# Half of the K stack transfers are issued by ScalarE's queue

## What is computed

```python
x = x + tanh(g_xattn) * xattn(layernorm(x), ctx, Wq, bq, Wk, bk, Wv, bv, Wo, bo)
x = x + tanh(g_ffn) * moe(layernorm(x), Wr, br, w1, b1, w2, b2, Wp1, bp1, Wp2, bp2)
```

## Time and profile before

| what | us |
|---|---|
| median of three runs | 2294.24 |
| the profiled execution | 2282.05 |
| its span on the core | 2280.3 |
| attention (by the stretches of the trace, about) | 0 to 1740 |
| experts (about) | 1760 to 2280 |
| TensorE busy, whole span | 2146.6 (94%) |
| ScalarE busy, whole span | 1162.3 (51%) |

### The profile page before, as it was taken

The page is one execution under the profiler, slowest core; times in us unless marked ns, Lnnn a source line. Parts: engine busy times, 40 slices in busy tenths (PEclk is TensorE's granted clock), DMA queues, the critical chain, the costliest instruction groups (busy, mean ns, idle before and its releaser), DMA issues. The chain is left out here.

```text
span 2280.3 us, 61866 instructions
## 1 busy us (share of the span) xinstructions
PE 2146.6 (94%) x23534; PEld 1870.1 (82%) x23534; DVE 1414.3 (62%) x3219; ACT 1162.3 (51%) x2765; POOL 803.2 (35%) x1200
## 2 busy tenths in 40 slices
PE   5899999999999999999999999999993799999994
PEld 4688888888888888888888888888872678888883
DVE  4777777777777777777777777777743111111114
ACT  1366666666666666666666666666651223333330
POOL 4323433433433433443343343344211133333331
PEclk9999999999999999999999999999986899999996
DMA  5555555555555555555555555555403686777775
GB/s 137 146 132 151 138 139 138 134 148 137 132 137 139 146 139 141 134 139 144 136 131 139 150 134 144 134 135 137 125 19 104 209 270 187 218 220 218 210 222 158
DMA packets 253683, 345.06 MB, mean 151 GB/s; under 512 B 90280, under 2 KB 170508, under 8 KB 253260
## 3 DMA queue, kind: packets, MB, share of 16 engines
q1 hardware_dynamic: 222716, 304.93, 50.2%
q0 software_dynamic: 20256, 23.21, 5.2%
q10 hardware_dynamic: 10416, 12.98, 1.7%
HBM read 155.83 MB, written 42.86 MB: 87 GB/s over the span
## 5 line engine op out<-in xcount | busy, mean ns | idle before, releaser
L569 DVE TENSOR_REDUCE max_part<-max_ps 100x1 f32<-100x512 f32 (+1 forms) x1536 | 994.7, 655 | 349.2 <-PE max_ps L809 325.2
L452 ACT ACTIVATE probs<-score_ps 128x400 f32<-128x400 f32 (+1 forms) x1536 | 753.6, 503 | 427.6 <-PE score_ps L792 419.5
L792 PE MATMUL score_ps<-q_stack,k_stack 97*128 97x200 f32 (+1 forms) x3072 | 618.4, 284 | 4.6 <-ACT probs L452 3.4
L809 PE MATMUL max_ps<-k_stack,q_stack 96*100 96x512 f32 (+1 forms) x1536 | 597.2, 389 | 10.1 <-DVE max_part L569 9.6
L792 PEld LDWEIGHTS score_ps<-q_stack,k_stack 97*128 97x128 f32 (+1 forms) x3072 | 476.0, 184 | 78.0 <-issue 32.8
L389 POOL TENSOR_TENSOR ctx_hi<-ctx_raw,zero_col 128x256 fp32r<-128x256 f32 (+1 forms) x384 | 213.3, 586 | 467.7 <-PE v_ps L823 427.4
L859 PE MATMUL pv_ps<-probs,v_ones 128*17 128x100 f32 x12288 | 307.5, 253 | 0.6 <-ACT probs L452 0.6
L859 PEld LDWEIGHTS pv_ps<-probs,v_ones 128*17 128x17 f32 x12288 | 261.9, 99 | 45.1 <-issue 37.5
L809 PEld LDWEIGHTS max_ps<-k_stack,q_stack 96*100 96x100 f32 x1536 | 257.2, 167 | 21.6 <-DVE max_part L569 16.3
L1222 ACT ACTIVATE hid<-h_ps,b_c 128x256 f32<-128x256 f32 x245 | 116.0, 474 | 311.3 <-PE h_ps L1378 311.3
L1122 POOL DMA_INDIRECT results_by_token<-y_t,slot x98 | 152.9, 1561 | 343.1 <-DVE y_t L1329 185.3
(11 more groups left out here) (186 smaller groups left out, 2289.5 us busy)
## 6 DMA issues: line engine op xcount, KB each, us to landing
k_stack<-k_hl SPq DMA_DIRECT2D x512, 128.0 KB, 2.6
w_raw<-in_w SPq DMA_DIRECT2D x98, 640.0 KB, 5.2
ctx_raw<-in_ctxT SPq DMA_DIRECT2D x64, 512.0 KB, 4.5
k_stack<-k_hl SPq DMA_DIRECT2D x512, 64.0 KB, 2.2
k_stack<-k_hl SPq DMA_DIRECT2D x256, 105.0 KB, 2.5
ctx_raw<-in_ctxT SPq DMA_DIRECT2D x32, 420.0 KB, 4.8
k_stack<-k_hl SPq DMA_DIRECT2D x256, 52.5 KB, 2.0
x_t<-rows_by_expert SPq DMA_DIRECT2D x49, 269.0 KB, 4.8
```

What stands on the lines that cost most here:

```text
L452: act.activation(probs[0:tw, n % PROBS, :], score_ps[n % 2][0:tw, 0:UH * SQ], ACT.Exp, scale=SCALE).then_inc(exp_done, 1)
L569: dve.tensor_reduce(max_part[b % 2][:, h, j:j + 1], max_ps[m % 2][0:SQ, 0:CW[j]], AX.X, ALU.max).then_inc(max_read, 1)
L792: ins = pe.matmul(score_ps[n % 2][0:TW[i], 2 * SQ * p:2 * SQ * (p + 1)], k_stack[b % 2][:, 2 * u + p, 128 * i:128 * i + TW[i]], q_stack[b ...
L809: pe.matmul(max_ps[m % 2][0:SQ, 0:CW[j]], q_stack[b % 3][0:96, h // 2, SQ * (h % 2):SQ * (h % 2) + SQ], k_stack[b % 2][0:96, h // 2, k0[j] ...
```

## The change

A helper `stack_keys` issues the two DMAs of each quarter that it is given. SP issues quarters 0 and 1, as before in its order. ScalarE issues quarters 2 and 3 in the same turn, after its exps 3 and ahead of the router's small Exps, behind the same two waits. The bytes, the shapes, the destinations and the semaphores are the same.

```diff
+        def stack_keys(eng, b, j, o, some):
+            for q in some:
+                dst = k_stack[b % 2][:, 4 * o + q, k0[j]:k0[j] + CW[j]].bitcast(F32)
+                src = k_hl[32 * q:32 * q + 32, o, :, 0:CW[j]].bitcast(F32)
+                eng.dma_start(dst[0:64, :], src).then_inc(k_stacked[j][o], 16)
+                eng.dma_start(dst[64:96, :], src[:, 1, :]).then_inc(k_stacked[j][o], 16)
...
                         wait(sp, k_read, KD * (NC * b + j) + o + 1)
                         wait(sp, score_done, UH * (NT * (b - 2) + TPC * (j + 1)))
-                        for q in range(4):
-                            dst = k_stack[b % 2][:, 4 * o + q, k0[j]:k0[j] + CW[j]].bitcast(F32)
-                            src = k_hl[32 * q:32 * q + 32, o, :, 0:CW[j]].bitcast(F32)
-                            sp.dma_start(dst[0:64, :], src).then_inc(k_stacked[j][o], 16)
-                            sp.dma_start(dst[64:96, :], src[:, 1, :]).then_inc(k_stacked[j][o], 16)
+                        stack_keys(sp, b, j, o, (0, 1))
...
                 exps(g, 3)
+                for j in range(NC):
+                    for o in range(KD):
+                        b = batch_at(g, 4 * j + 2 * o)
+                        if b is not None:
+
+                            wait(act, k_read, KD * (NC * b + j) + o + 1)
+                            wait(act, score_done, UH * (NT * (b - 2) + TPC * (j + 1)))
+                            stack_keys(act, b, j, o, (2, 3))
```

## The result

The changed kernel takes 2413.82 us (median of four runs, 2411.51 to 2421.67), the kernel before on the same chip 2294.33. The ratio is 1.053, with an interval of 1.051 to 1.055: 120 us slower, where 144 had been forecast (2438, range 2336 to 2560).

What follows compares the result with a forecast made beforehand. TensorE was taken as the bound in the steady stretch, with ScalarE following it. Stalls of +152 us and the fill's -8 gave +144 on the median of 2294.24, so 2438 us, range 2336 to 2560.

Steps and rivals of the forecast that it cites:

- The price of an issue: On ScalarE's queue: one K stack DMA issue takes 0.64 us, bounds 0.39 to 0.65.
- rival 1: ScalarE's issues are cheap or overlap, the fill's gain remains: 2292, or 2286 with exps 3 overlapped; chance 0.11.
- The chain: ScalarE's work from scores 3 to the odd turn's scores 2: 1.43 us without issues, 3.99 with four.
- exps 3 until the next instruction can begin 0.40: Part of the chain on ScalarE: the issues begin only 0.40 us after exps 3 starts.
- that case: ScalarE's sequencer issues while exps 3 still runs: 0.40 off each chain, stalls of 79 us, total 2365.
- The stalls: TensorE waiting at scores 2 of odd turns: 0.835 us a turn, 182 turns, +152 us.
- I add nothing: After the stall at scores 2: no second stall before the next turn's scores 0, though no slack, so 0 us.
- The fill: Pipeline start: ScalarE's `k_hl` waits less for K stack DMAs, -8 us, bounds 0 and -17.
- Rival 2: SP's and ScalarE's queues hold each other up: 2548, about 2904 if every issue collides; chance 0.18.
- The lock of the Trainium skill: Cited under rival 2: a sequencer locks a shared descriptor block, lock wait inside the profiled time; no size of its own.
- Rival 3: TensorE's stalls lower its granted clock in the steady stretch: at 0.93, +113, about 2551; chance 0.05.

Runs made afterwards that it cites:

- e4: Changed kernel, but ScalarE issues only quarter 3, two issues, behind exps 3; 2288.39 us, ratio 0.9984 to the kernel before.
- e3: Changed kernel with ScalarE's four issues split, two behind exps 1 of the even turn, two behind exps 1 of the odd turn; 2291.39 us, ratio 1.0002.
- e6: Changed kernel with two issues behind exps 3 and the other two behind exps 0 of the odd turn; 2321.37 us, ratio 1.014.
- e9: Changed kernel with all eight issues back on SP, ScalarE keeping only the two added waits; 2282.51 us against 2281.60, ratio 1.0006.
- e1: Changed kernel, but ScalarE issues only in turns before 20, SP all eight later; 2287.05 us against 2291.60 for the kernel before, ratio 0.9987.
- e7: Changed kernel with three of the eight issues, not four, on ScalarE at the same place; 2316.42 us, ratio 1.012 to the kernel before.
- e2: Changed kernel with ScalarE's four issues in one piece behind exps 1 of the even turn, not behind exps 3; 2467.99 us, ratio 1.078.
- e5: As e2, but from turn 20 SP holds its own four issues until ScalarE's exps 3 of the turn; 2417.65 us, ratio 1.055.
- e8: Changed kernel with all eight issues on ScalarE at the same place, none on SP; 3201.17 us, ratio 1.399 to the kernel before.
- e10: Changed kernel with ScalarE's four issues in one piece behind exps 1 of the odd turn, ahead of the keys; 2503.84 us against 2281.60, ratio 1.098.

## Why the prediction was right

**Direction and mechanism.** ScalarE got four issues in one piece ahead of exps 0, and TensorE waited for `probs` through the two score buffers. e4, e3 and e6 show that the piece does it and not the number of issues, e9 that the waits do not, e1 that the fill gains on its own.

**The price of an issue** was taken from SP's rows and ScalarE's 610 ns as 0.64 us with the gap to the next. Measured: 606 and 618 ns, four in 2.54 us in the median. The 349 ns of the issues with an address from a register were no guide, and rival 1 fell. The prediction set them aside for that address, which was not the right reason: SP's store of 100 x 256 (L347 of the kernel before) has a fixed address and took 340 ns in the median. What makes such issues short is not shown.

**The chain** was set at 3.99 us and is 3.66 in the median of a plain turn. The step that was wrong is "exps 3 until the next instruction can begin 0.40": the issue starts together with exps 3. The prediction named that case and priced it at 79 us of stalls. The 0.10 rather than 0.04 us between the last issue and the next Exp takes 0.06 of this back.

**The stalls** came to 0.73 us a turn (a batch takes 56.0 us where it took 51.65), where 0.835 were forecast, but not of the same parts. Scores 2 are late by 0.56 in the mean, against 0.84 forecast and 0.44 for a start with exps 3. Of the 0.12 above that, half is the 0.06 just named, and the rest are single long issues (the median piece is 2.54 us and the mean 2.62). The step "I add nothing" for what follows scores 2 missed 0.17: 0.09 at scores 3, and 0.08 a turn that falls almost all in the one turn of six behind `pv_out`, the place that e7 shows, whose cause is open. Two errors of opposite sign made the sum look better than its parts: too much by the overlap, too little by the tail. That the time lies so near the forecast is partly luck.

**The fill** was forecast at -8 us and is -5.7 (e1: -7.7). ScalarE's three waits for the K stack, 17.2 us in the earlier trace rows, became one, and of the 12.1 us saved there about half arrived at the first Exp:

```profile
ACT k_hl L504 <- DMA k_stack<-k_hl: 5.1, 1, 5.1
```

**Rival 2**, two queues that hold each other up, is hardly seen in the changed kernel. In the turn where SP is at work during 2.3 of the 2.7 us of the piece, the piece takes 2.54 us in the median (2.71 in the mean), and 2.52 (2.58) where SP overlaps it by 0.2. The lock of the Trainium skill (Perfetto Trace Analysis, DMA Instruction (HWDGE)) would have shown as longer issues there. e2 does show joint holds, at a place where both queues start at once, and e5 puts their worth at 0.25 us a turn. **Rival 3**, the clock, did not come in the changed kernel with stalls of under 1 us (1.00), but did in e8 with 3 us and more (0.86).

**No version beats the kernel before by much.** e1 and e4 are 0.13% and 0.16% faster, with intervals that end just under 1. SP's queue, which the change relieves, bounds the kernel in the fill alone.

## What to carry to other kernels

An instruction queue that also feeds the bound engine is not free room, even if its engine is idle half of the time: an issue of a DMA took ScalarE 0.6 us, and four in a row were longer than what two buffers of scores could cover. Ask how long the longest run of work is between two instructions for which the bound engine waits, and compare it with the distance that the buffers allow, turn by turn. Spread over that distance, the same issues cost a tenth, and what one gains by moving them is only what the old queue held up, here 6 us of fill.

## What the runs showed that I had not expected

- A DMA issue on ScalarE's queue starts with the ACTIVATE ahead of it, 0.01 us before its start in the rows of the changed kernel (1149.26 and 1149.27) and 0.06 after it in the median of e2 and e10, not when that ACTIVATE ends. The ACTIVATE behind the issues starts 0.05 to 0.10 us after the last of them in the medians.
- DMA issues that start within 2.5 us of the beginning of TensorE's 64 short matmuls are long more often, on both queues (66 of 400 over 0.75 us on SP before, 168 of 455 on ScalarE in e2, against 26 of 900 and 14 of 131 elsewhere), and two issues that are held at once end at once (109 of 127 in e2). What holds them is open.
- The granted clock stood at 1.00 in the changed kernel and at 0.99 in e2 and e10, with stalls of TensorE of about 1 us in every second turn, and fell to 0.86 on average in e8 with stalls above 3 us.
- In about half of the batches of e7 TensorE's signal for one half of the values comes some 1.8 us after the end of these matmuls in the rows, and `v_ones` starts only then. The same turn costs e4 and the changed kernel some 10 us each. Nothing in the profile says why.
